# A decoder layer with two experts per token on one core: seven tiles in the first token set, routing in more steps, later norms on ScalarE

## The reference, cut to what matters

```python
h = layernorm(x, eps=1e-5) * gamma + beta                        # x: (2, 1024, 256)
keys, values = h @ Wk.T + bk, h @ Wv.T + bv
key_att = keys @ Wka.T + bka
kw = exp(key_att / 16);  kw = kw / cumsum(kw, axis=1)
x = _layernorm(x + cumsum(kw * keys, axis=1) * values)           # x1

Q, K, V = split(x @ W_q.T), split(ctx @ W_k.T), split(ctx @ W_v.T)   # 16 heads of 16; ctx has 77 rows
scores = where(mask, -inf, Q K / 4)
x = _layernorm(x + merge(softmax(scores) V) @ W_o.T)             # x2

logits = flat @ router_w.T + router_b                            # flat: (2048, 256), 8 experts
topk_vals, topk_idx = top_k(logits, 2);  topk_w = softmax(topk_vals)
for e in range(8):
    cw = sum(where(topk_idx == e, topk_w, 0.0), axis=-1)
    y = gelu(flat @ w1[e].T + b1[e]) @ w2[e].T + b2[e]           # 256 -> 1024 -> 256
    out = out + y * cw[:, None]
x = _layernorm(x + _layernorm(out + flat, eps=1e-12) * ln_w + ln_b)
```

## Time and profile before

| what | value |
|---|---|
| median of 3 runs | 539.31 us (537.64 to 541.08) |
| the profiled execution | 541.87 us |
| its span, first to last instruction | 540.1 us |
| mean granted TensorE clock in it | 0.972 |
| TensorE busy | 501.5 us |
| VectorE, ScalarE, GpSimd busy | 374.5, 251.0, 260.0 us |

### The profile page before, as it was taken

One profiled execution on the slowest core, in us unless ns is written; L12 is line 12 of the kernel. 1 busy time (PEld: TensorE's weight loads), 2 busy tenths in 40 slices (PEclk: granted clock), 3 DMA queues, 4 the chain that ended last, 5 costly groups with the idle time before them and its releaser, 6 DMA issues.

```text
span 540.1 us, 10882 instructions
## 1 busy us (share of the span) xinstructions
PE 501.5 (93%) x3286; PEld 450.1 (83%) x3286; DVE 374.5 (69%) x1114; ACT 251.0 (46%) x835; POOL 260.0 (48%) x369
## 2 busy tenths in 40 slices
PE   6789999989999869988999999999999999999991
PEld 5657888878888757878799999999999999999980
DVE  3767979858677886537977667665667656766774
ACT  3436666756666436653244334344443334444320
POOL 4534222212212240418267666665676756766565
PEclk9879999999999979999999999999999999999997
DMA  8109930835575625406546666666666665666420
GB/s 231 12 4 302 348 113 6 273 112 180 176 234 172 198 74 210 152 21 229 183 127 214 220 225 206 202 192 194 211 220 227 217 208 202 203 215 231 143 51 1
DMA packets 57280, 93.69 MB, mean 173 GB/s; under 512 B 12018, under 2 KB 49017, under 8 KB 52103
## 3 DMA queue, kind: packets, MB, share of 16 engines
q1 hardware_dynamic: 49975, 79.91, 44.3%
q0 software_dynamic: 5616, 12.82, 7.8%
q10 hardware_dynamic: 1632, 0.27, 0.3%
HBM read 65.64 MB, written 30.18 MB: 177 GB/s over the span
## 4 chain that ended last, share of the span: by engine, by line
PE 35%; issue 19%; POOL 19%; DVE 16%; DMA 7%; ACT 2%; POOLq 1%; ACTq 0%; SPq 0%; DVEq 0%
PE psum_b L1495 8%; PE psum_v L1628 6%; PE psum_a L1594 6%; DMA work<-weighed_outputs,routing 4%; POOL routing L772 4%; POOL out L776 4%; POOL work L768 3%; POOL work L763 3%; PE psum_m L1646 2%; POOL front_then_w_ring L729 2%; DMA weighed_outputs<-work 2%; PE psum_m L1495 2%; DVE routing L1364 2%; PE psum_c L1615 2%; PE psum_a L1739 1%
## 5 line engine op out<-in xcount | busy, mean ns | idle before, releaser
L969 ACT ACTIVATE front_then_w_ring<-psum_a,front_then_w_ring 128x128 f32<-128x128 f32 x160 | 45.8, 369 | 73.3 <-PE psum_a L1739 73.3
L879 ACT ACTIVATE work<-psum_a,score_max 128x77 f32<-128x77 f32 x256 | 62.4, 335 | 34.4 <-DVE score_max L1136 34.3
L1739 PEld LDWEIGHTS psum_a<-front_then_w_ring 128*128 128x128 f32 x640 | 74.4, 192 | 3.9 <-issue 3.0
L1739 PE MATMUL psum_a<-front_then_w_ring 128*128 128x128 f32 x640 | 75.1, 275 | 2.6 <-ACT front_then_w_ring L959 2.0
L969 ACT ACTIVATE front_then_w_ring<-psum_b,front_then_w_ring 128x128 f32<-128x128 f32 x152 | 43.3, 369 | 69.1 <-PE psum_b L1739 69.1
L1762 PE MATMUL psum_v<-expert_w,front_then_w_ring 128*128 x320 | 72.7, 380 | 0.1
L1739 PEld LDWEIGHTS psum_b<-front_then_w_ring 128*128 128x128 f32 x608 | 70.9, 192 | 0.9
L1739 PE MATMUL psum_b<-front_then_w_ring 128*128 128x128 f32 x608 | 71.1, 275 | 0.0
L1762 PE MATMUL psum_c<-expert_w,front_then_w_ring 128*128 x304 | 68.8, 379 | 0.0
L1762 PEld LDWEIGHTS psum_v<-expert_w,front_then_w_ring 128*128 128x128 f32 x320 | 59.3, 190 | 7.6 <-issue 0.4
L1762 PEld LDWEIGHTS psum_c<-expert_w,front_then_w_ring 128*128 128x128 f32 x304 | 56.3, 190 | 6.9
(11 more groups left out here) (242 smaller groups left out, 887.9 us busy)
## 6 DMA issues: line engine op xcount, KB each, us to landing
front_then_w_ring<-in_w1b SPq DMA_DIRECT2D x39, 1028.0 KB, 4.9
weighed_outputs<-routing SPq DMA_DIRECT2D x16, 1024.0 KB, 6.6
expert_w<-in_w SPq DMA_DIRECT2D x8, 1024.0 KB, 10.3
weighed_outputs<-work SPq DMA_DIRECT2D x37, 128.0 KB, 2.3
token_rows<-front_then_w_ring SPq DMA_DIRECT2D x16, 128.0 KB, 1.8
second_buffers<-in_x SPq DMA_DIRECT2D x4, 256.0 KB, 4.9
token_rows<-routing SPq DMA_DIRECT2D x1, 1024.0 KB, 5.4
front_weights_then_tail<-in_b SPq DMA_DIRECT2D x1, 1024.0 KB, 8.4
```

The source lines that it names most:

```text
L879: last = act.activation(prob[:, u % RING_U, at_k:at_k + SC], pa[:, H % 2, g * SC:(g + 1) * SC], ACT.Exp, bias=smax[:, j % 2, head:head + 1])
L969: last = act.activation(hidT[t % 2][:, c, :], src[:, n, q * P:(q + 1) * P], ACT.Gelu, bias=bias[:, c:c + 1])
L1739: last = pe.matmul(dst[:, n, q * P:(q + 1) * P], w1[:, k, c * P:(c + 1) * P], xtT[t % 2][:, k, :], start=(k == 0), stop=(k == KD - 1))
```

## The change

- The first token set has seven tiles and the second nine, and the first set owns seven slot tiles (`FIRST`).
- The first set's routing was in steps 45, 46 and 49; it is spread over steps 41, 44, 47, 50, 51 and 52, `RANKS_STEP` is 50, and its marks are made in steps 53 to 56. `weigh(0)` is in step 48.
- Marks are made for a group of neighbouring token tiles by three operations (`mark_rows`), where each pair had two of its own. The second set has four groups, of 5, 4, 5 and 4 pairs.
- From the fourth piece of the pipeline on, `x1_normalise`, and `x2_normalise` for all but the last two tiles, are ScalarE's. GpSimd makes a shift for them from mean and reciprocal root, with three operations for a norm where it had one.
- Pieces 3 and 4 of the x1 pipeline have sum and norm a step earlier; from piece 5 on the turn of x1 and the queries are a step later.
- The first gathers are issued in steps 58, 60 and 62, two rows are turned in steps 61 and 63, and the first expert tile's matmuls go to psum_b. The change-over has another order on each engine; the second set's marks are multiplied ahead of `up(5, 0)`, and the gathers of tiles 7, 8 and 9 come out of their former order.

```diff
-FIRST = 8
+FIRST = 7
...
-SETS = ((0, TILES // 2), (TILES // 2, TILES // 2))
+SETS = ((0, FIRST), (FIRST, TILES - FIRST))
...
+MARK_GROUPS = tuple(tuple((c * n + a, c * n + b) for c in range(TOPK) for a, b in ((0, (n + 1) // 2), ((n + 1) // 2, n))) for _, n in SETS)
...
+BY_ACT = 3
...
-            return pc[:, 1, 0:D] if t < 2 else pm[:, 0:D]
+            return pb[:, 1, t * D:(t + 1) * D] if t < 2 else pm[:, 0:D]
...
+                pool.tensor_scalar(x2_drop[:, j:j + 1], x2_mv[:, j, 0:1], -1.0, None, ALU.mult).then_inc(x2_drop_made, 1)
...
+                pool.tensor_tensor(x2_shift[:, j:j + 1], x2_drop[:, j:j + 1], x2_rstd[:, j:j + 1], ALU.mult).then_inc(x2_rstd_ready, 1)
...
-                if H == RANKS_STEP - 1:
+                if H == RANKS_STEP - 2:
                     weigh(0)
-                if H == RANKS_STEP + 1:
+                if H == RANKS_STEP + 2:
                     map_tiles(0)
                     rows_of_choice(0)
-                if H == CHUNKS * STEPS - 6:
+                if H == RANKS_STEP + 8:
                     first_rows_ready()
                     load_tile(0)
                     load_tile(1)
-                if H == CHUNKS * STEPS - 2:
+                if H == RANKS_STEP + 10:
                     load_tile(2)
+                if H == RANKS_STEP + 12:
                     load_tile(3)
...
+                if t == FIRST - 4:
+                    return (FIRST,)
+                if t == FIRST - 3:
+                    return (FIRST + 1, FIRST + 2)
+                return (t + AHEAD,) if t + AHEAD < SLOT_TILES else ()
...
-                if t == 0:
+                if t == 2:
...
+                if piece_at("x1", H) is not None and piece_at("x1", H) >= BY_ACT:
+                    x1_normalise(piece_at("x1", H))
+                if H % QUADS == 2 and H >= 10:
+                    x2_normalise((H - 10) // QUADS)
+                if H == CHUNKS * STEPS - 2:
+                    turned_rows(0)
...
+            def x2_normalise(t):
+                j = t % 2
+                act.wait_ge(x2_rstd_ready, t + 1)
+                if t >= 2:
+                    act.wait_ge(x2_out[j], t // 2 * 16)
+                    act.wait_ge(x2T_mm, t - 1)
+                act.activation(x2c[:, j, :], r2[:, j, :], ACT.Identity, scale=x2_rstd[:, j:j + 1],
+                               bias=x2_shift[:, j:j + 1]).then_inc(x2_ready, 1)
...
+            turned_rows(1)
             output_features(TILES - 3)
             act.preload_act_table(ACT.Gelu)
-            turned_rows(0)
+            hidden(0, 0)
             turned_heads(TILES - 1)
-            hidden(0, 0)
-            turned_rows(1)
             hidden(0, 1)
             output_features(TILES - 2)
+            hidden(1, 0)
+            hidden(1, 1)
+            turned_rows(2)
             act.wait_ge(map_ready, MAPS)
             weighed_bias(0)
-            hidden(1, 0)
             output_features(TILES - 1)
-            hidden(1, 1)
-            turned_rows(2)
+            hidden(2, 0)
+            hidden(2, 1)
+            turned_rows(3)
             weighed_bias(1)
-            for t in range(2, SLOT_TILES):
+            weighed_bias(2)
+            for t in range(3, SLOT_TILES):
                 hidden(t, 0)
                 hidden(t, 1)
...
                 dve.wait_ge(o_mm, t + 1)
+                if t >= 2:
+                    dve.wait_ge(x2_ready, t - 1)
...
-                if H == (CHUNKS - 1) * STEPS - 3:
-                    first_choice(0)
-                if H == (CHUNKS - 1) * STEPS - 2:
+                if H == RANKS_STEP - 9:
+                    first_top(0)
+                if H == RANKS_STEP - 6:
+                    first_hot(0)
+                if H == RANKS_STEP - 3:
                     second_choice(0)
                 if H == RANKS_STEP:
                     first_map()
+                if H == RANKS_STEP + 1:
+                    map_of(tbend, spare, FIRST, 0.0)
+                    place_later()
+                if H == RANKS_STEP + 2:
                     place(0)
-                if H == RANKS_STEP + 9:
+                if H == RANKS_STEP + 8:
...
-                dve.tensor_scalar(where, cols, part_n[:, c, t:t + 1], None, ALU.is_equal)
-                dve.tensor_scalar(which, cols, part_n[:, TOPK + c, t:t + 1], token1[:, t:t + 1], ALU.is_equal,
+                slot_numbers = cols.rearrange("p (a m) -> p a m", a=1).to_broadcast(over)
+                dve.tensor_tensor(at_pos[n][:, first_pair:end], slot_numbers, over_slots(part_n[:, c, ts]), ALU.is_equal)
+                then(dve.tensor_tensor(at_col[n][:, first_pair:end], slot_numbers, over_slots(part_n[:, TOPK + c, ts]), ALU.is_equal))
+                dve.tensor_tensor(at_col[n][:, first_pair:end], at_col[n][:, first_pair:end], over_slots(token1[:, ts]),
                                   ALU.mult).then_inc(pos_ready, 1)
...
-            route_logits(TILES - 1)
-            first_choice(LAST)
-            second_choice(LAST)
             indices(2)
             weigh_output(0)
             add_input(0)
+            route_logits(TILES - 1)
+            first_top(LAST)
+            first_hot(LAST)
+            second_choice(LAST)
+            dve.memset(token_of[:, P:COLS], 0.0)
             rest_map()
             ranked(LAST)
             place(LAST)
-            for i in range(SET_PAIRS[LAST] // 2):
-                mark(LAST, i)
             dve.wait_ge(ln_in, 2 * 16)
-            indices(3)
             weigh_output(1)
             add_input(1)
             sum_row(0)
-            for i in range(SET_PAIRS[LAST] // 2, SET_PAIRS[LAST]):
-                mark(LAST, i)
-            later_map()
+            mark_rows(LAST, *MARK_GROUPS[LAST][0])
             row(inner_norm(0))
+            indices(3)
             sum_row(1)
-            dve.memset(token_of[:, P:COLS], 0.0)
-            dve.wait_ge(pos_mm, LAST + 1)
-            dve.tensor_tensor(token_of[:, 0:P], table_psum(LAST), first_token_of, ALU.add).then_inc(table_ready, 1)
+            mark_rows(LAST, *MARK_GROUPS[LAST][1])
+            mark_rows(LAST, *MARK_GROUPS[LAST][2])
...
+                if t == 2:
+                    mark_rows(LAST, *MARK_GROUPS[LAST][3])
+                    later_map()
+                if t == FIRST - 4:
+                    dve.wait_ge(pos_mm, LAST + 1)
+                    dve.tensor_tensor(token_of[:, 0:P], table_psum(LAST), first_token_of, ALU.add).then_inc(table_ready, 1)
...
-                if H == RANKS_STEP + 7:
+                if H == RANKS_STEP + 6:
                     mark_pairs(0)
+                if H == CHUNKS * STEPS - 3:
+                    turn_rows(0)
+                if H == CHUNKS * STEPS - 1:
+                    turn_rows(1)
...
+            up(0, 0)
             weigh_values(CHUNKS * UNITS - 1)
             output_features(TILES - 3)
-            turn_rows(0)
-            up(0, 0)
+            up(0, 1)
             turn_heads(TILES - 1)
             route_logits(TILES - 3)
-            up(0, 1)
-            turn_rows(1)
+            up(1, 0)
             project_out(TILES - 1)
             output_features(TILES - 2)
-            up(1, 0)
+            up(1, 1)
             route_logits(TILES - 2)
-            output_features(TILES - 1)
-            up(1, 1)
-            route_logits(TILES - 1)
+            pe.wait_ge(r2_ready, TILES)
+            turn_rows(2)
             pe.wait_ge(map_ready, MAPS)
             pe.wait_ge(w2_in, E * 16)
             down(0)
+            output_features(TILES - 1)
+            up(2, 0)
+            route_logits(TILES - 1)
+            up(2, 1)
             pe.wait_ge(lg_ready, TILES)
             ranks(LAST)
-            pe.wait_ge(r2_ready, TILES)
-            turn_rows(2)
-            for t in range(2, SLOT_TILES):
+            turn_rows(3)
+            down(1)
+            for t in range(3, SLOT_TILES):
+                if t == FIRST - 2:
+                    pe.wait_ge(placed, 3 * LAST + 1)
+                    mark_pairs(LAST)
                 up(t, 0)
                 up(t, 1)
```

163 lines of the change are left out of this document (96 added, 67 removed).

## The result

The changed kernel takes **542.83 us** (median of 16 runs, 541.20 to 548.05) against 538.09 us for the kernel before (16 runs). The ratio is 1.0067, with an interval of 1.0046 to 1.0088, so it is slower by 0.67%, or 3.6 us. (The ratio is not the quotient of the two medians, which are 4.7 us apart.) Measured again beside later experiments it was 1.0044 (1.0019 to 1.0070). The forecast was 1.3 us faster. 542.83 lies in the range, but the sign was wrong: there is a small loss where a small gain was forecast.

A forecast was written before the change was run, and what follows sets the result against it. TensorE bounds the kernel, so only its idle time and low clock before about 285 us can change. 5.7 + 0.5 - 4.9 = 1.3 us gained, 539.31 to 538.0 us; forecast 535 to 540.5 (43%), range 530 to 545.

The forecast's parts named there:

- Routing spread over steps: First set's routing among attention steps: 10.0 us of idle time and low clock recovered, less new waits, 5.7 us gained.
- the wait at step 51: Attention phase: TensorE waits 2.1 us for exponentials behind ScalarE's `x2_normalise(10)`, which waits for GpSimd in `weigh(0)`.
- steps 53 to 55: Mark groups beside a residual or the heads overfill VectorE's steps: 2.2 us of TensorE waits in three pieces.
- The later slots of x1's turn and queries have the same matmuls: nothing: Attention phase, x1 pipeline: moving turn and queries to later steps costs or gains nothing.
- hidden: Attention phase: ScalarE's norms, 0.59 us each, cost no time, as ScalarE is busy about 12 of 16.47 us.
- The change-over: Attention to experts: today's 4.2 us idle becomes 2.5 at last ranks plus 1.2 at first rows; 0.5 us gained (-1 to +2.5).
- The later marks: Second set's marks ahead of `up(5,0)`: TensorE waits 4.2 us, then 2.8 at `turn_rows(7)`; less today's 2.1, 4.9 us lost.
- VectorE's chain: From the end of the last ranks to the fourth mark group: VectorE needs 23.35 us against TensorE's 19.1.
- the slow rival: Later marks: GpSimd and VectorE slow twelve two-tensor operations by 0.5 us each, 6 us; 544.0 us, 546 with low clock; 15%.
- the sum holds no waits of VectorE for GpSimd: Later marks: the 23.35 us sum leaves out such waits, an argument against marks costing no wait; no size given.
- The gather's chain: From the fourth mark group to tile 7's rows landed: 14.05 us, against TensorE's 11.25 to `turn_rows(7)`.
- No wait at the marks: Fast rival, later marks: with a VectorE chain of 19 us marks cost nothing; 8.3 us gained, 531.0 us; 24%.

The follow-up runs named there:

- old_pieces: Changed kernel with the x1 pipeline's sum, norm, turn and queries back in their old steps, norms still on ScalarE; 538.43 us, 0.9978 to the kernel before.
- marks_by_pairs: Changed kernel with the second set's marks made pair by pair, by the old two one-tensor operations; 542.88 us, 1.0044 to the kernel before.
- weigh_later: Changed kernel with the second set's fourth mark group, table and tile 7's gather earlier, and `weigh(0)` in step 50; 536.86 us, 0.9935 to the kernel before.
- tile7_first: weigh_later with the second set's map and table ahead of tile 2's sum, tile 7's gather ahead of tile 2's root; 536.15 us, 0.9920 to the kernel before.

## Why the prediction was wrong, point by point

**Routing spread over steps, 5.7 us forecast: right.** It was 4.5 to 6.1 by the two profiles of each kernel, with what the moved steps cost in the same stretch already off it (old_pieces gains 6.8 to 7.3 there). The two places named were the places: the wait at step 51 was forecast at 2.1 us, behind `weigh(0)` and a norm of ScalarE, and was 1.45; steps 53 to 55 were forecast at 2.2 and took 1.47 of wait and, in the first profile alone, 1.6 of low clock (0.83 over 9.55 us of work in 202 to 212).

**"The later slots of x1's turn and queries have the same matmuls: nothing": the first step that failed.** Same matmuls, but in their old steps they stood ahead of late exponentials and covered them, and the moved ones left TensorE idle there. Ahead of step 41 the kernel lost 1.4 us net, where the forecast had nothing, and old_pieces shows some 3.6 us for the moved steps in all (3.8 by the waits). The same paragraph had ScalarE's norms "hidden", by its share of busy time; it did not ask where in ScalarE's queue they stand. At 72.7 us the norm of x1 (1.08 us) is directly ahead of the exponentials, for a wait of 0.92.

**The change-over, 0.5 us forecast: 1.4 to 2.8.** Better than forecast, and in part beyond its upper bound of 2.5. The wait at the last ranks was 1.8 for 2.5. `turn_rows(0)` waited 1.43 us for its gather, as named (1.2), in one profile, and has no wait of note in the other.

**The later marks, 4.9 us lost (3 to 6.5) forecast: 7.4 to 8.0, the second step that failed.** The mechanism was right, the term too small. TensorE waited 6.7 us instead of 4.2. VectorE's chain, 23.35 us by the working, took 26.3 from the last ranks (246.81) to the last mark's end (273.12); the operations had the forecast durations (0.82 and 0.68 for a mark operation), and the rest is the two collisions with GpSimd (1.8 us) and two waits of VectorE of 0.5 and 0.6 us, one for base rows. Both had been seen: the collision as the slow rival, and "the sum holds no waits of VectorE for GpSimd" as an argument against the fast one. Neither was put into the sum. Then low clock took 2.7 us (1.8 in the second profile), as the text allowed, and tile 7's rows 0.4 more on top, where the two were to stand for each other. The gather's chain itself was forecast at 14.05 us from the fourth group, and took that (273.12 to 287.17).

**The rivals.** "No wait at the marks" fell. "Slower by GpSimd and VectorE" was right in kind at 1.8 us, not 6: the price comes with a wide addition of GpSimd and not with each operation of VectorE. The row that it was priced from (L1234, 0.66 for 0.17 us) and the one behind it (L1228, 0.77) both lie at one such addition of the kernel before; together they are 1.0 us slow, and they were counted as 0.5 us for every operation. Of the two operations that were slow in the changed kernel one was a mark operation. The addition, in the profile of before:

```profile
249.10 0.74 POOL L768 TENSOR_TENSOR work<-front_then_w_ring,front_weights_then_tail 128x256 f32<-128x256 f32 x1
```

**The sum.** With the measured terms: 4.5 to 6.1 gained, 1.4 lost in the early steps, 1.4 to 2.8 gained, 7.4 to 8.0 lost, and about 0.5 behind tile 7: between 4.0 and 0.4 us lost by these ends (0.7 to 3.9 from step 5 to the end of the span in the profiles), against 3.6 by the ratio of the times. The base played no part in the sign: the execution behind the rows had a start 2.5 us dearer than the next, but no term was read from its start. It made the miss in time larger by 1.2 us, since the median of three that the 538.0 starts from, 539.31, is that much above the median of sixteen.

## What to carry to other kernels

Where a wait is forecast on one chain, look for the next chain that ends at the same engine a little later: here the marks and the gather behind them hid each other, and moving one alone made the kernel 5 us slower. A move of "the same work" by one step among steps of 2 us is not free until it is checked what each queue has in that step, and which wait the work was covering where it stood: it was the one part of the sum that was costed without a row. And where a chain is bound by one engine, add what the rows show of its neighbours (collisions, waits for DMAs) to the sum instead of keeping them for a rival.

## What the runs showed of the hardware

In two places of each profile of the changed kernel a VectorE operation over two tensors at which GpSimd began a two-tensor addition over 256 columns (0.74 us) took 0.9 us longer (0.48 to 1.38 us, 0.82 to 1.72). It took its usual time when the addition was one column wide. With operations over one tensor in the same places (marks_by_pairs) two in a row were slow, by 0.5 to 0.6 us each. At the next addition (275.55) the operation beside it kept its 0.48 us, so such an addition does not always cost, and what decides is open. Two-tensor mark operations beside a DMA issue of GpSimd (262.60 to 264.06 in the changed kernel) took their usual 0.68 to 0.82 us.

The start of the same program came at two paces: step 2 of the attention phase at 38.0 us in one profile of the changed kernel and 43.3 in the other, with the granted clock at 1.00 and at 0.74 in 28 to 43 us; in the two profiles of the kernel before it was 38.6 and 42.9, at 1.00 and 0.76. Low clock behind one and the same wait is not certain either: behind the 1.5 us at the marks the 32 matmuls of `up(5, n)` took 3.79 us in weigh_later's profile and 5.42 in that of tile7_first.
